# A decoder layer on one core: three PSUM banks for scores and two for maxima, other order tables, and the odd stacks' constant rows issued after the first shift

## The reference, cut to what matters

```
x = x + self_attention(layernorm(x))        # 16 heads of 16, causal, with ALiBi bias
x = x + cross_attention(layernorm(x), ctx)  # 16 heads of 16 over 120 context tokens
x = x + tanh(layernorm(x) @ W @ A1 @ A2 + bias)
```

## Time and profile before

| | |
|---|---|
| median of three runs | 2411.53 us (2410.28 to 2416.39) |
| the profiled execution | 2413.22 us, span 2411.4 us |
| granted TensorE clock, mean | 0.979 |
| busy: PE, PE weight load | 93%, 77% |
| busy: DVE, ACT, POOL | 71%, 59%, 30% |

### The profile page before, as it was taken

The page is one execution under the profiler, slowest core; times in us unless marked ns, Lnnn a source line. Parts: engine busy times, 40 slices in busy tenths (PEclk is TensorE's granted clock), DMA queues, the critical chain, the costliest instruction groups (busy, mean ns, idle before and its releaser), DMA issues.

```text
span 2411.4 us, 67050 instructions
## 1 busy us (share of the span) xinstructions
PE 2235.1 (93%) x22072; PEld 1850.9 (77%) x22072; DVE 1710.2 (71%) x3710; ACT 1416.4 (59%) x3066; POOL 719.4 (30%) x1371
## 2 busy tenths in 40 slices
PE   3489999999999999999999999999999999999985
PEld 2367887887788788788878878887887888788774
DVE  3167777777777777777777778777777877777762
ACT  2246666666666666666666666666666666666651
POOL 1223233233333323323332332333233233323321
PEclk9699999999999999999999999999999999999996
DMA  7333443443343344334334433433443343344320
GB/s 126 76 81 104 115 109 95 111 109 97 99 118 105 97 111 109 96 100 118 104 98 111 109 93 102 115 103 101 111 109 89 106 114 101 105 111 109 89 81 22
DMA packets 167370, 244.83 MB, mean 102 GB/s; under 512 B 22176, under 2 KB 90512, under 8 KB 164248
## 3 DMA queue, kind: packets, MB, share of 16 engines
q1 hardware_dynamic: 165660, 244.22, 38.2%
q10 hardware_dynamic: 1664, 0.01, 0.1%
HBM read 53.13 MB, written 33.56 MB: 36 GB/s over the span
## 4 chain that ended last, share of the span: by engine, by line
PE 74%; DVE 8%; POOL 4%; DMA 4%; issue 4%; SPq 2%; ACT 2%; DVEq 0%; POOLq 0%; ACTq 0%
PE ps_misc L534 13%; PE ps_misc L548 13%; PE ps_score L622 7%; PE ps_max L605 5%; PE ps_score L632 5%; PE ps_score L623 4%; PE ps_attend L647 4%; PE ps_misc L677 4%; DVE neg_max_s L962 4%; PE ps_max L593 4%; PE ps_misc L518 3%; PE ps_misc L692 3%; PE ps_attend L666 2%; DMA q_stack<-neg_max_t_s 2%; PE ps_misc L559 2%
## 5 line engine op out<-in xcount | busy, mean ns | idle before, releaser
L805 ACT ACTIVATE probs<-ps_score 128x384 f32<-128x384 f32 x1024 | 476.0, 494 | 177.4 <-PE ps_score L623 174.2
L962 DVE TENSOR_REDUCE neg_max_s<-ps_max 128x2 f32<-128x512 f32 (+1 forms) x768 | 479.5, 680 | 5.5 <-PE ps_max L587 4.1
L812 ACT ACTIVATE xprobs<-ps_score 120x512 f32<-120x512 f32 x512 | 292.4, 597 | 251.9 <-PE ps_score L632 213.8
L622 PE MATMUL ps_score<-q_stack,k_stack 128*128 128x256 f32 x1024 | 343.0, 345 | 46.4 <-DMA q_stack<-neg_max_t_s 42.3
L1095 POOL TENSOR_SCALAR ve_LN<-mv_LN 128x2 f32<-128x2 f32 x192 | 37.0, 193 | 1152.1 <-DVE mv_LN L984 1146.5
L970 DVE TENSOR_REDUCE neg_max_x<-ps_max 128x4 f32<-128x480 f32 x512 | 317.0, 651 | 25.7 <-PE ps_max L605 14.1
L623 PE MATMUL ps_score<-q_stack,k_stack 128*128 128x256 f32 x1024 | 279.6, 281 | 0.0
L622 PEld LDWEIGHTS ps_score<-q_stack,k_stack 128*128 128x128 f32 x1024 | 194.1, 190 | 92.3 <-DMA q_stack<-neg_max_t_s 58.5
L632 PE MATMUL ps_score<-xq_stack,xk_stack 128*120 128x256 f32 x1024 | 201.7, 309 | 3.7 <-DMA xq_stack<-neg_max_t_x 2.8
L1121 POOL TENSOR_TENSOR res<-res,chain_n 128x512 f32<-128x512 f32 x64 | 81.7, 1276 | 412.6 <-ACT chain_n L850 412.6
L593 PE MATMUL ps_max<-k_stack,q_stack 127*128 127x256 bf16 x1024 | 195.7, 282 | 4.1 <-DVE neg_max_s L962 0.6
(11 more groups left out here) (147 smaller groups left out, 5394.0 us busy)
## 6 DMA issues: line engine op xcount, KB each, us to landing
k_stack<-k_nat SPq DMA_DIRECT2D x192, 256.0 KB, 3.6
q_stack<-q_nat SPq DMA_DIRECT2D x192, 256.0 KB, 3.7
xq_stack<-q_nat SPq DMA_DIRECT2D x192, 256.0 KB, 3.7
xk_stack<-scr_xk SPq DMA_DIRECT2D x192, 128.0 KB, 2.7
x_in<-in_x SPq DMA_DIRECT2D x64, 256.0 KB, 2.7
scr_xk<-k_nat SPq DMA_DIRECT2D x32, 512.0 KB, 3.0
out_y<-res SPq DMA_DIRECT2D x64, 256.0 KB, 2.2
ctx_in<-in_ctx SPq DMA_DIRECT2D x32, 240.0 KB, 3.0
```

The lines of the kernel that those rows point to most:

```text
L622: pe.matmul(bk[:, 0:T], ks[:, h, P:T], qs[:, h, :], start=True, stop=True)
L805: act.activation(probs[:, h % 8, :], bank_of("SCORE", i, b, h)[:, P:4 * P], ACT.Exp)\
L812: act.activation(xprobs[0:C, at:at + 2, :], blocks(bank_of("XSCORE", i, b, u))[0:C], ACT.Exp).then_inc(sem("xprobs_ready"), 1)
L962: dve.tensor_reduce(o, ins, AX.X, ALU.max, negate=True).then_inc(sem("max_taken"), 1)
```

## The change

Five things change.

1. `SCORE`'s first matmul takes queries 128 to 255 alone: 128 columns and not 256. With it the steps rows are laid per half of the tokens (`NSTEP` 2, other powers of two), still in 64 partitions.
2. `RINGS`: two banks for maxima, three for scores.
3. The `ORDER` tables are others. A step is cut at another place of the cycle, so the same item can stand with another offset.
4. `comes_first` differs by engine. SP does `MAX_STACK` of sequence 0 before `other_rows`. POOL does the clears before `LN1` of sequence 1.
5. At the start, the ALiBi rows are loaded before the weights of Q and K, and the waits for the bias vectors move from the preparation to the first item that uses them.

The core of the diff:

```
-NSTEP = 4
-UP = [2.0 ** (57 - 38 * p) for p in range(NSTEP)]
-DOWN = [0.0] + [-2.0 ** (38 * p - 82) for p in range(1, NSTEP)]
-BEYOND = -2.0 ** 70
+NSTEP = 2
+UP = [[2.0 ** (70 - 90 * a - 45 * p) for p in range(NSTEP)] for a in range(2)]
+DOWN = [[0.0, -2.0 ** (90 * a - 55)] for a in range(2)]
+BEYOND = [-2.0 ** (90 * a - 10) for a in range(2)]
...
     "PE": (
-        ("SCORE", 0, 4), ("ATTEND", 0, 0), ("SCORE", 0, 5), ("XOUT_T", -2, 0), ("SCORE", 0, 6),
...
+        ("XSCORE", -1, 2), ("XSCORE", -1, 3), ("OUT_T", 0, 0), ("MAX", 1, 4), ("CTX_T", 0, 0),
...
-RINGS = {"max": 3, "score": 2, "attend": 1, "misc": 2}
+RINGS = {"max": 2, "score": 3, "attend": 1, "misc": 2}
...
-FIRST_STEP, LOOP_FROM, LOOP_TO, END_STEP = -2, 6, 62, NSEQ + 2
+FIRST_STEP, LOOP_FROM, LOOP_TO, END_STEP = -2, 8, 62, NSEQ + 3
...
-        def comes_first(kind, b):
-
-            return kind in ("LOAD_X", "LOAD_CTX", "LN1", "LN1_T", "K", "Q") or \
-                kind in ("K_STACK", "Q_STACK") and b == 0
+        def comes_first(name, kind, b):
+
+            if name == "SP":
+                return kind not in ("K_STACK", "Q_STACK", "XK_STACK") or b == 0 and kind != "XK_STACK"
+            if name == "POOL":
+                return b == 0
+            return kind in ("LN1", "LN1_T", "K", "Q")
...
-            for n in ["q", "k", "alibi", "f1", "f0", "f2", "v", "o", "xq", "xk", "xv", "xo"]:
+            for n in ["alibi", "q", "k", "f1", "f0", "f2", "v", "o", "xq", "xk", "xv", "xo"]:
...
                     if name == "xq":
+                        if isinstance(i, int) and b == 0:
+                            sp.wait_ge(sem("rows_set1"), 16 * 12)
...
-                pe.matmul(bk[:, 0:T], ks[:, h, P:T], qs[:, h, :], start=True, stop=True)
+                pe.matmul(bk[:, P:T], ks[:, h, P:T], qs[:, h, P:T], start=True, stop=True)
                 pe.matmul(bk[:, T:2 * T], ks[:, h, 0:P], qs[:, h, :], start=True, stop=True)\
...
-            act.wait_ge(sem("alibi_copied"), 1)
-            act.wait_ge(sem("b_loaded"), 16 * 9)
-            act.wait_ge(sem("b_scaled"), 1)
...
+                    if isinstance(i, int) and kind in ("K", "Q") and b == 0:
+                        act.wait_ge(sem("alibi_copied"), 1)
+                        act.wait_ge(sem("b_loaded"), 16 * 9)
+                        act.wait_ge(sem("b_scaled"), 1)
...
-            dve.wait_ge(sem("b_loaded"), 16 * 9)
-            dve.tensor_scalar(bcol["q"][:, :], bcol["q"][:, :], SCALE["q"], None, ALU.mult)
...
+                    if isinstance(i, int) and kind == "LN1_T" and b == 0:
+                        scale_biases()
...
-            pool.wait_ge(sem("b_loaded"), 16 * 9)
```

## The result

The changed kernel takes 2410.92 us (median of 20 runs, 2406.97 to 2414.43), the kernel before 2414.83 us in 20 runs on the same chips (2410.02 to 2418.25). The ratio is 0.9984, with a 95% interval of 0.9977 to 0.9991: 4 us faster, of 36 that the sum had (the forecast was made against the median of three runs, 2411.53; that of 20 is 3.3 us higher). The profiled execution of the changed kernel has a span of 2408.3 us and a mean clock of 0.985.

What follows compares the result with a forecast made beforehand. PE was taken to bound the loop, while all engines stand idle at the start. From 2413.2 us, 31 for the start, 5 for the narrow matmul and 0 for the loop gave 2377, leaned to 2374; range 2342 to 2403.

Steps and rivals of the forecast that it cites:

- The start: Before the loop: 28.7 + 3.5 - 1.2 = 31 us saved in all, from 24 to 35.
- The shift first: Start: sequence 0's shift DMAs go ahead of the constant rows, `SCORE` 0 at 68.5 instead of 97.2, 28.7 us saved.
- The other two terms: Start: later bias waits and earlier ALiBi rows save 3.5 us (2.5 to 6); `V` between `MAX` 8 and 9 costs 0, at most 1.
- The narrow matmul: `SCORE`'s first matmul with half its columns: 0 to 10 us saved, 5 taken, as the weight load bounds it.
- The rule by columns: `SCORE`'s narrow matmul: N / 2.4 + 2.5 ns, 53 ns saved each, 55 us in all; as a rival 2318, chance 0.06.
- The walk of the loop: PE's new order and banks: work between producer and consumer against the chain beside it, gains and losses summing to 0.0 per sequence.
- `XMAX_T` to `XSCORE` 0: Cross shift: the way needs 3.2 us, 2.3 of work stand between; 0.9 lost, less 0.2 of old `MAX` bank wait: 0.7.
- Banks. With three for scores, `XSCORE` waits less for the exponential: some 0.3 saved: Cross scores in the loop: a third score bank saves some 0.3 us per sequence; two banks for maxima cost nothing.
- the old order lost about as much: `SCORE` 3 needs `SCORE` 0's bank back: some 0.3 lost, about as much as before with two banks, so nothing.
- The closing step: After the sum of 2377: late waits absorb earlier ones that the walk counts singly, so 1.5 us less, 2374.
- the cross shift decides: Rival: PE waits 0.9 us longer before `XSCORE` 0 in each sequence and savings elsewhere don't come; 2432 us, chance 0.13.
- The walk's own bound: Loop: guesses good to some 0.15 each give +-0.45 us per sequence, +-28 us over 63 periods.

## Why the prediction was wrong, by its steps

Forecast 2374, measured 2410.9. The start held, the loop didn't.

**The start: right, two of its terms by luck.** -31 us in the sum, -31.0 measured by itself. `SCORE` 0 came at 63.2, a little before the 64 to 69 given, `MAX` 1 at 85.2, within 82 to 88. The low clock of 60 to 100 us is half gone (0.79). The rows and `K_STACK` collide a little, as allowed for: `MAX` 1 comes 22.0 us behind `SCORE` 0, where it was 19.0. The shift first was sized right. The other two terms missed their ranges and offset each other: with the old order and the new start `MAX_T` comes at 57.15 us, 7.7 before the 64.85 of the earlier trace rows, for which I had 3.5 and 6 at most; in the changed kernel it comes at 59.71, 2.6 us later. The chain of waits there runs over `V`, now between `MAX` 8 and 9, for which I had 0 to 1.

**The narrow matmul: the size about right, its sign in the profile wrong.** 5 us in the sum, some 3 by the periods, not told from nothing by the times. I expected 0.11 to 0.12 us from line 627 to 628; it is 0.06, and the distance to the next pair is longer. The pace of a pair, not of a matmul, was the thing to name. The rule by columns that the prediction set against the load is given in the Trainium skill, "TensorE: Matmul & The Clock Gate", section "Back-to-back issue gap", for a matmul by itself, and its 55 us should not have been set beside a stream in which each matmul has a load of its own; the runs show nothing of them.

**The walk of the loop: wrong, 0.0 in the sum and +0.5 us measured.** The periods differ by 0.47 us; with the wide matmul, that is, for order and banks alone, 35.75 stands against 35.23, so +0.52. To see which terms failed I cut the loop at the same items in both kernels and took from each stretch the same price of work (per matmul 0.05 us for the short bf16 ones, 0.11 for the long, 0.12 for those of `K`, `Q`, `V` and scores, 0.11 for transposes, 0.057 and 0.04 for `ATTEND`, 0.07 for `XATTEND`, 0.14 for `XSCORE`). What is left is waiting and changes between kinds, in us per sequence. The prices are rough, so a stretch by itself is good to some 0.1 us; in the differences most of that falls out.

| stretch | before | after | difference | predicted |
|---|---|---|---|---|
| `XMAX_T` to `XSCORE` 0 | 0.35 | 1.13 | +0.78 | +0.7 |
| `XSCORE` 0 to `SCORE` 0 | 1.46 | 1.32 | -0.14 | -0.5 |
| `SCORE` 0 to the score behind `LN1_T` | 0.43 | 0.73 | +0.30 | 0 |
| the rest, to `XMAX_T` | 1.57 | 1.10 | -0.47 | -0.2 |
| sum | 3.81 | 4.28 | +0.47 | 0.0 |

- `XMAX_T` to `XSCORE` 0 was sized right; only its place is different. I expected a wait for the DMA; more than half of it (0.47 us) shows as a wait for ACT at `HEADS_OUT`. The wait before `XSCORE` 0 (0.35 us) goes unnamed in the profile for most sequences (it is put down to "issue"), and the experiments show that it is the shift's.
- The step that failed first is "Banks. With three for scores, `XSCORE` waits less for the exponential: some 0.3 saved". It saved nothing that can be found. PE's list of waits before has none at `XSCORE`, so there was little to save. By the prices above, what is left from `XSCORE` 0 to 5 is 0.16 us before and 0.18 after, and from `XSCORE` 5 to 7, where `OUT_PROJ`, `XK`, `V` and `MAX` items now stand between, it grew from 0.13 to 0.39: changes between kinds of matmul, which I had not moved with the items. Part of these come from the next stretch, to `SCORE` 0, which with `LN2_T` and `XQ` in it went down by 0.43, where 0.2 was foreseen.
- The second is a term that the walk doesn't have at all, and so put at nothing: the wait of `XHEADS_OUT` 1 for the `misc` bank that `XQ` filled. `SCORE` 3 itself came out as said, "the old order lost about as much": what is left from `SCORE` 0 to `SCORE` 3 is 0.39 us before and 0.44 after. The 0.3 lie behind it, where `XHEADS_OUT` 1 waits for the bank of `XQ` (1177.91 above). I had moved `XQ` ahead of the scores and priced only its start. No run undid this placement, so that it is `XQ`'s bank is read from the trace and not shown by an experiment.
- In the rest the saving was larger than I gave it. These stretches were not tested one by one.

In short, the savings and the losses of order and banks were put at nothing together, and the runs show 0.5 us per sequence lost. What each single term gave is worked out from distances in the trace. Of the terms of the walk only the first stretch was changed by itself in runs.

**The closing step.** "I lean by 1.5 us" towards faster because a late wait absorbs earlier ones. The runs show the opposite direction of the same rule: what is saved ahead of a wait is absorbed too. In the old order 0.3 us at `SCORE` 0 became 0.14 in the period. Of the rivals, "the cross shift decides" named the mechanism: +0.78 there, and the savings elsewhere didn't come in full. Its price assumed that none came (2432), and the run lies between it and the forecast, at a loss of some 0.5 us per sequence where 0.57 was the point of no gain.

**The range.** The walk's own bound, +-0.45 us, was passed: +0.52. Its upper end by itself, 2377 + 28, is 2405, and the range ended below that, at 2403. A walk with many terms, half of them without a row, needed more room, above all as two steps failed to the same side.

## What to carry to other kernels

When a reordering takes cover out of a stretch that ends in a fixed way (copy, issue, DMA), put the length of that way against the work that is left; that term came out within 0.1 us here. Savings elsewhere count only where a wait in a row shrinks. When an item is moved, follow its bank too: a score's bank came back 1.1 us behind the score's start, more than twice the exponential's 0.5, and `XQ`'s bank held up a transpose two items later. Before rearranging cover, look whether the way itself can be shortened: one DMA instead of two for a small row brought 11 us in the old order and 24 in the new, more than the whole change did.

## What the runs showed that I had not expected

Two small DMAs, issued one behind the other by SP, take 1.15 to 1.19 us of issue, one of the same data 0.55 to 0.57. The DMA view gives the median from issue to landing (number of issues, KB each, us), in the old loop with two DMAs

```profile
q_stack<-neg_max_t_s SPq DMA_DIRECT2D x128, 8.0 KB, 1.8
```

and with one:

```profile
q_stack<-neg_max_t_s SPq DMA_DIRECT2D x64, 16.0 KB, 2.1
```

Each of the two lands 1.8 us after its issue, but the second starts some 0.6 later; the one lands after 2.1. That is the 0.3 us of `SCORE` 0. The Trainium skill, "DMA: Bandwidth & Descriptors", section "Rules for kernel authors", says that two transfers to disjoint halves are not worth making and should be one; it speaks of halves of the partitions. Here the two read 16 partitions each and write two halves of one partition's row, with the same answer: the runs show 11 and 24 us for joining them.

Unexpected too was how closely order and banks are bound: one bank moved either way, with the order left as it was, took 1.08 and 1.07 times as long.
